# A four-bank rotation of the expert pre-activations in PSUM, sharing two banks with the mask broadcast

## The chip, the cores and the metric

The kernel runs on the 8 NeuronCores of one Trainium2 chip, as two dies of four cores each. Every core gets two of the sixteen sequences, that is 4096 rows of 1024 features, and all the weights; the cores exchange nothing. The metric is the device time in microseconds (us) of the slowest core, lower is better. TensorE is called PE below, its weight load PEld, VectorE DVE, ScalarE ACT, GpSimd POOL and SyncE, which issues most of the DMAs, SP.

## What is computed

The layer is a gated linear recurrence beside a mixture-of-experts feed-forward block with four experts and a hard choice of one for each token. Cut to what matters here:

```python
xn = layernorm(x)
s = xn + recurrence(rmsnorm(xn))              # forget / input / output projections, scan over time
logits = xn @ W_router
expert_idx = argmax(logits)                   # one of E = 4 experts for each token
h = einsum('th,ehi->tei', xn, W1) + b1        # H = 1024, I = 4096
h = gelu(h)
intermediate = einsum('te,tei->ti', onehot(expert_idx), h)
y = layer_norm(intermediate @ Wo + bo + xn)
out = x + s * silu(y)
```

## The kernel before

A core works in two blocks. Block A (the first 750 us or so) casts the weights to bf16 in DRAM, normalizes, projects, scans, and stores xn and s in bf16. Block B does the feed-forward part and is where the change is. It works through NT = 8 tiles of TT = 512 tokens, with features on partitions and tokens on the free axis.

The hard choice is turned into masking of the input: `maskedA` holds four copies of the tile's xn, copy e multiplied by the 0/1 mask of expert e, so that one accumulation over 4 experts x 8 slices of the features gives the pre-activation of the chosen expert. For each of IC = 32 slices of the 4096 intermediate features, called **groups** below (index `i_abs`), PE runs 32 matmuls of 128x128 by 128x512 (L621) and one matmul of 4 rows that adds the bias through the masks `mask4_bf` (L628), all into one PSUM bank, `pre[b]` with `b = i_abs % 2`. ACT reads that bank with one Gelu into `interA` (L784). The semaphore `pre_R<b>` counts finished groups of a bank (PE to ACT), `pre_F<b>` counts finished Gelus (ACT to PE): PE may start group i when the Gelu of group i-2 is done. The group's 1 MB of W1 comes through `w1sl`, two slots, loaded by SP.

After the 32 groups of tile t, PE runs `mask_prep(t + 1)`, which makes the masks of the next tile: four small transposes into `pmb2` (L588); DVE copies the result to `mask4_bf` (L717, in `mask_block`), after waiting for the last group of the tile; two matmuls (L594, L596) spread the masks of experts 0 and 1 over all partitions in `pmb` and `pmb2`; ACT copies both to `mb_bf` (L766, L767, in `mb_evacs`); then the same for experts 2 and 3 (L599, L601; L769, L770). Only then does PE start the second matrix product of tile t (L642, 8 output slices of 32 matmuls, accumulated in `y2a` and `y2b` in turn), which reads all of `interA`. DVE meanwhile builds `maskedA` of the next tile (L723) and then follows y2 with casts and squares (L740, L742). Sums for the layer norm go through `pmu` and `psq` (L655, L660), and in the middle of the next tile's groups PE transposes the finished product back (`emit_ptr`, L571, L578).

Each engine runs its own instruction list strictly in the order written. ACT's list for a tile is: the 32 Gelus, with a square root ahead of group 4 (`sqrtp`) and eight Silus ahead of group 12 (`silup`), both for the tile before; a drain; `mb_evacs(t + 1)`; eight reads of y2 (L794). A bank of PSUM holds 512 fp32 values in each partition, and block B allocates eight of them: `pre0`, `pre1`, `y2a`, `y2b`, `pmu`, `psq`, `pmb`, `pmb2`. All eight are used, `pmb` and `pmb2` only in `mask_prep`.

In SP's list of a tile the 32 loads of `w1sl` wait for `sl_F` (a group's weights used up), the 8 of `wosl` for `wo_F`; the load of the xn after the next and with it the first two `w1sl` loads of a tile wait for the last y2 of the tile before.

Of the kernel before, what the change touches and what calls it, by code (L numbers as in the profile page):

```python
# [28 lines left out]
def build_core(debug=False):  # L29
# [24 lines left out]
    with es:  # L54
# [20 lines left out]
            "pj_R0", "pj_F0", "pj_R1", "pj_F1",  # L75
            "ss_o", "vb_R0", "vb_F0", "vb_R1", "vb_F1",
            "sv_s", "bar",
            "s_xb0", "s_xb1", "s_sb", "sl_R0", "sl_R1", "sl_F", "wo_R0", "wo_R1", "wo_F",
            "s_lgR", "sv_lgF", "sv_mtm", "s_mtR", "sv_m4", "s_mbR", "ss_mb", "sv_msk",
            "pre_R0", "pre_F0", "pre_R1", "pre_F1", "s_predone", "ss_int",  # L80
            "y2_R0", "y2_F0", "y2_R1", "y2_F1", "s_wodone", "ss_y3",
            "sv_y3bf", "mu_R", "mu_F", "sq_R", "sq_F", "sv_var", "ss_sqrt",
            "sv_z", "ss_g", "sv_p", "s_pdone", "sv_out", "st_out",
# [3 lines left out]
        def ti(instr, name, k=1):  # L87
            instr.then_inc(SM[name], k)
            return instr

        def W(eng, name, val):
            if val > 0:
                eng.wait_ge(SM[name], val)
# [378 lines left out]
        with contextlib.ExitStack() as esB:  # L472
# [31 lines left out]
            pmb2_bf = pmb2.bitcast(BF16)  # L504
            pmu_bf = pmu.bitcast(BF16)
            psq_bf = psq.bitcast(BF16)

            y3bf = p_bf
            y3sq = g_bf
# [4 lines left out]
            with nc.Block() as blockB:  # L514
# [47 lines left out]
                def _(te):  # L562
# [20 lines left out]

                    def mask_prep(tau):
                        W(te, "ss_mb", 2 * tau)
                        ins = None
                        for sub in range(SUB):
                            ins = te.transpose(  # L588
                                pmb2_bf[0:4, sub * 128:(sub + 1) * 128],
                                mask_all[:, (tau * SUB + sub) * E:(tau * SUB + sub + 1) * E],  # L590
                                ident_bf[:, :])
                        ti(ins, "s_mtR", 1)
                        W(te, "sv_m4", tau + 1)
                        te.matmul(pmb[:, :], sel_bf[:, 0:128], mask4_bf[:, :],  # L594
                                  start=True, stop=True)
                        ti(te.matmul(pmb2[:, :], sel_bf[:, 128:256], mask4_bf[:, :],  # L596
                                     start=True, stop=True), "s_mbR", 1)
                        W(te, "ss_mb", 2 * tau + 1)
                        te.matmul(pmb[:, :], sel_bf[:, 256:384], mask4_bf[:, :],  # L599
                                  start=True, stop=True)  # L600
                        ti(te.matmul(pmb2[:, :], sel_bf[:, 384:512], mask4_bf[:, :],  # L601
                                     start=True, stop=True), "s_mbR", 1)

                    mask_prep(0)
                    for t in range(NT):
                        W(te, "sv_msk", t + 1)
                        for grp in range(NG):
                            if grp == NG // 2 and t > 0:
                                emit_ptr(t - 1)
                            gi = t * NG + grp  # L610
                            W(te, "sl_R%d" % (gi % 2), 16 * (gi // 2 + 1))
                            for il in range(G):
                                i_abs = grp * G + il
                                b = i_abs % 2
                                pr = t * IC + i_abs
                                W(te, "pre_F%d" % b, pr // 2)
                                first = True
                                for e in range(E):
                                    for k in range(KC):
                                        off = ((k * E + e) * G + il) * 128  # L620
                                        ins = te.matmul(  # L621
                                            pre[b][:, :], w1sl[gi % 2][:, off:off + 128],
                                            maskedA[:, (e * KC + k) * TT:(e * KC + k + 1) * TT],
                                            start=first, stop=False)
                                        first = False
                                        if il == G - 1 and e == E - 1 and k == KC - 1:
                                            ti(ins, "sl_F", 1)
                                ti(te.matmul(pre[b][:, :],  # L628
                                             b1t_bf[:, i_abs * 128:(i_abs + 1) * 128],
                                             mask4_bf[:, :], start=False, stop=True),  # L630
                                   "pre_R%d" % b, 1)
# [35 lines left out]
                def _(v):  # L667
# [45 lines left out]

                    def mask_block(tau):
                        W(v, "s_mtR", tau + 1)
                        W(v, "pre_R1", 16 * tau)
                        ti(v.tensor_copy(mask4_bf[:, :], pmb2_bf[0:4, 0:TT]), "sv_m4", 1)  # L717
                        W(v, "ss_mb", 2 * (tau + 1))
                        W(v, "s_xb%d" % (tau % 2), 16 * (tau // 2 + 1))
                        ins = None  # L720
                        for e in range(E):
                            for k in range(KC):
                                ins = v.tensor_tensor(  # L723
                                    maskedA[:, (e * KC + k) * TT:(e * KC + k + 1) * TT],
                                    xn_b[tau % 2][:, k * TT:(k + 1) * TT],
                                    mb_bf[:, e * TT:(e + 1) * TT], OP.mult)
                        DR(v, "sv_msk")
# [22 lines left out]
                def _(sc):  # L750
# [22 lines left out]
                    for t in range(NT):  # L773
                        sc.drain()
                        W(sc, "y2_R1", 4 * t)
                        for i_abs in range(IC):
                            if i_abs == 4 and t > 0:
                                sqrtp(t - 1)
                            if i_abs == 12 and t > 0:
                                silup(t - 1)  # L780
                            b = i_abs % 2
                            pr = t * IC + i_abs
                            W(sc, "pre_R%d" % b, pr // 2 + 1)
                            ti(sc.activation(interA[:, i_abs * TT:(i_abs + 1) * TT],  # L784
                                             pre[b][:, :], AF.Gelu), "pre_F%d" % b, 1)
                        DR(sc, "ss_int")
                        if t + 1 < NT:
                            mb_evacs(t + 1)
                        W(sc, "st_out", 16 * t)
                        for h in range(KC):  # L790
                            wi_ = t * KC + h
                            b = h % 2
                            W(sc, "y2_R%d" % b, wi_ // 2 + 1)
                            ti(sc.activation(y3[:, h * TT:(h + 1) * TT], y2[b][:, :],  # L794
                                             AF.Identity, bias=bo_cm[:, h:h + 1]),
                               "y2_F%d" % b, 1)
                        DR(sc, "ss_y3")
# [39 lines left out]
```

## Time and profile before

| what | value |
|---|---|
| time, median of 2 runs | 3296.91 us (3293.29 and 3300.54) |
| the profiled execution: time | 3300.92 us |
| its span on the slowest core (core 4) | 3299.0 us |
| spans of the eight cores | 3267.0 to 3299.0 us |
| mean granted TensorE clock, by core | 0.948 to 0.955 of full speed |
| PE busy, share of the span | 88% |
| DVE, ACT, POOL busy | 21%, 14%, 6% |
| mean busy share of the 16 DMA engines in block B | about 40% |

All rows are of one execution, on its slowest core. The span runs from the first to the last instruction of that core. PE's matmuls are pipelined, so the duration of a single one (about 380 ns) is longer than the distance from one to the next (about 219 ns); distances between starts are what counts. The granted clock is 1.00 at 2.4 GHz and 0.50 at 1.2 GHz. An idle time is put down to the instruction that ended it.

### The profile page before, as it was taken

The numbers are of one execution on the slowest core, as the hardware profiler recorded it, in microseconds if no ns is written. First come the engines' busy times: TensorE is split into PE (matmuls) and PEld (weight loads), VectorE is DVE, ScalarE is ACT, GpSimd is POOL, SyncE is SP. The second block draws the span as 40 slices with busy tenths as digits, with TensorE's granted clock in tenths as the row PEclk, the third lists the DMA queues.
The fourth block names the chain that finished last, engine by engine and source line by source line (L and its number), as shares of the span: only waits on it lengthen the run. The fifth ranks groups of instructions, "written<-read, shape, count | busy, mean of one in ns | idle before, by whom it ended". The sixth has DMA issues, their size and how long they took to land.

```text
span 3299.0 us, 32665 instructions; the slowest of 8 cores (3267.0 to 3299.0 us)
## 1 busy us (share of the span) xinstructions
PE 2891.8 (88%) x13376; PEld 1266.9 (38%) x13376; DVE 705.2 (21%) x1289; ACT 470.1 (14%) x733; POOL 211.7 (6%) x285
## 2 busy tenths in 40 slices
PE   0247778786999999999999999999999999999994
PEld 0113333332444444344444444444444444444442
DVE  0326666662002200310121012002200210021003
ACT  1122222210001110011102011101110111102001
POOL 1015252400000000000000000000000000000000
PEclk9878889898999999999999999999999999999997
DMA  9999999904444444444354434443444444344432
GB/s 133 105 131 124 128 123 148 142 29 164 143 141 166 153 159 161 153 142 164 128 190 141 154 139 179 151 156 139 180 155 147 180 137 161 141 166 141 161 145 76
DMA packets 262385, 476.14 MB, mean 144 GB/s; under 512 B 204700, under 2 KB 204700, under 8 KB 216988
## 3 DMA queue, kind: packets, MB, share of 16 engines
q1 hardware_dynamic: 88640, 408.99, 37.8%
q0 software_dynamic: 173600, 65.07, 18.4%
q8 instruction: 109, 1.79, 0.2%
q14 instruction: 36, 0.29, 0.0%
HBM read 482.44 MB, written 81.79 MB: 171 GB/s over the span
## 4 chain that ended last, share of the span: by engine, by line
PE 73%; DVE 1%; ACT 1%; DMA 1%; issue 1%; DVEq 0%; ACTq 0%; SPq 0%; POOL 0%; POOLq 0%
PE pre L621 55%; PE y2a L642 7%; PE y2b L642 7%; PE pre L628 2%; DMA w1sl<-w1s 1%; PE pmu L655 0%; DVE y L674 0%; DVEq L96 0%; DVE y L678 0%; PE psq L660 0%; PE pmu L571 0%; DVE maskedA L723 0%; PE y2b L647 0%; PE y2a L647 0%; ACT g_bf L760 0%
## 5 line engine op out<-in xcount | busy, mean ns | idle before, releaser
L621 PE MATMUL pre<-maskedA,w1sl 128*128 128x512 bf16 x8192 | 1823.3, 381 | 15.8 <-DVEq L96 12.4
L621 PEld LDWEIGHTS pre<-maskedA,w1sl 128*128 128x128 bf16 x8192 | 784.2, 98 | 988.7 <-issue 88.6
L784 ACT ACTIVATE interA<-pre 128x512 bf16<-128x512 f32 x256 | 152.8, 597 | 1721.0 <-PE pre L628 1720.9
L642 PE MATMUL y2a<-interA,wosl 128*128 128x512 bf16 x1024 | 238.7, 394 | 1.1 <-ACTq L96 1.1
L642 PE MATMUL y2b<-interA,wosl 128*128 128x512 bf16 x1024 | 226.2, 379 | 0.0
L717 DVE COPY mask_bf<-pmb 4x512 bf16<-4x512 bf16 x8 | 3.3, 412 | 951.7 <-PE pmb L588 951.7
L162 POOL DMA_DIRECT2D w1s<-w x256 | 188.0, 776 | 277.9 <-issue 277.9
L456 PE MATMUL pj<-xn_fm,wfT 128*128 128x512 bf16 x512 | 127.1, 410 | 83.8 <-ACT f_fm L243 58.5
L558 POOL DMA_DIRECT2D out<-y x8 | 6.0, 745 | 2631.9 <-DVEq L96 2631.9
L417 PE MATMUL trA<-ident_bf,xn_tm 128*128 128x128 bf16 x256 | 34.5, 278 | 141.9 <-DVEq L96 105.3
L642 PEld LDWEIGHTS y2a<-interA,wosl 128*128 128x128 bf16 x1024 | 102.5, 101 | 133.5 <-issue 21.9
L456 PE MATMUL pj<-xn_fm,wiT 128*128 128x512 bf16 x512 | 125.8, 409 | 28.8 <-DVE v_bf L325 16.4
L642 PEld LDWEIGHTS y2b<-interA,wosl 128*128 128x128 bf16 x1024 | 100.2, 98 | 120.9
L740 DVE CAST p_bf<-y 128x512 bf16<-128x512 f32 x64 | 27.3, 427 | 452.2 <-ACT y L794 450.1
L456 PE MATMUL pj<-xn_fm,woT 128*128 128x512 bf16 x512 | 121.8, 402 | 0.0
L456 PEld LDWEIGHTS pj<-xn_fm,wfT 128*128 128x128 bf16 x512 | 52.5, 104 | 157.4 <-issue 107.7
L711 DVE TENSOR_TENSOR p_bf<-s_b,g_bf 128x4096 bf16<-128x4096 bf16 x8 | 18.3, 2292 | 385.2 <-ACT g_bf L760 385.2
L628 PE MATMUL pre<-mask_bf,b1t_bf 4*128 4x512 bf16 x256 | 98.3, 384 | 0.0
L723 DVE TENSOR_TENSOR maskedA<-xn_b,mb_bf 128x512 bf16<-128x512 bf16 x256 | 86.6, 423 | 35.0 <-ACT mb_bf L770 35.0
L456 PEld LDWEIGHTS pj<-xn_fm,wiT 128*128 128x128 bf16 x512 | 52.2, 104 | 98.6 <-issue 49.1
L417 PEld LDWEIGHTS trA<-ident_bf,xn_tm 128*128 128x128 bf16 x256 | 23.7, 127 | 147.8 <-issue 146.5
L700 DVE TENSOR_TENSOR y<-y,mu_rep 128x512 f32<-128x512 f32 x64 | 39.2, 686 | 185.0 <-ACT rstd_rep L755 185.0
(114 smaller groups left out, 1240.0 us busy)
## 6 DMA issues: line engine op xcount, KB each, us to landing
w1sl<-w1s SPq DMA_DIRECT2D x256, 1024.0 KB, 4.8
wosl<-wos SPq DMA_DIRECT2D x64, 1024.0 KB, 5.0
w1s<-w POOLq DMA_DIRECT2D x256, 128.0 KB, 14.2
x_a<-x SPq DMA_DIRECT2D x8, 2048.0 KB, 14.7
x_b<-x SPq DMA_DIRECT2D x8, 2048.0 KB, 16.8
out<-y POOLq DMA_DIRECT2D x8, 2048.0 KB, 7.8
wos<-wo POOLq DMA_DIRECT2D x8, 1024.0 KB, 46.3
xnbf_s<-xn_fm SPq DMA_DIRECT2D x8, 1024.0 KB, 23.6
```

The lines of the kernel that those rows point to most:

```text
L162: ti(g.dma_start(out=dst, in_=src), "gp_cst", 16)
L417: ins = te.transpose(trA[p_][:, sub * 128:(sub + 1) * 128], xn_tm[:, sub * D + k * 128: sub * D + (k + 1) * 128], ident_bf[:, :])
L456: ins = te.matmul(pj[b][:, :], wT[:, k * D + c * 128: k * D + (c + 1) * 128], xn2_fm[:, k * TT:(k + 1) * TT], start=(k == 0), stop=(k == K ...
L558: ti(g.dma_start(out=dsto, in_=srco), "st_out", 16)
L621: ins = te.matmul(pre[b][:, :], w1sl[gi % 2][:, off:off + 128], maskedA[:, (e * KC + k) * TT:(e * KC + k + 1) * TT], start=first, stop=False)
L628: ti(te.matmul(pre[b][:, :], b1t_bf[:, i_abs * 128:(i_abs + 1) * 128], mask4_bf[:, :], start=False, stop=True), "pre_R%d" % b, 1)
L642: ins = te.matmul(y2[b][:, :], wosl[wi_ % 2][:, ic * 128:(ic + 1) * 128], interA[:, ic * TT:(ic + 1) * TT], start=(ic == 0), stop=False)
L700: v.tensor_tensor(y3[:, k * TT:(k + 1) * TT], y3[:, k * TT:(k + 1) * TT], mu_rep[:, :], OP.subtract)
L711: ti(v.tensor_tensor(p_bf[:, :], s_b[:, :], gsl(0, KC), OP.mult), "sv_p", 1)
L723: ins = v.tensor_tensor(maskedA[:, (e * KC + k) * TT:(e * KC + k + 1) * TT], xn_b[tau % 2][:, k * TT:(k + 1) * TT], mb_bf[:, e * TT:(e + 1 ...
L740: v.tensor_copy(y3bf[:, h * TT:(h + 1) * TT], y3[:, h * TT:(h + 1) * TT])
L784: ti(sc.activation(interA[:, i_abs * TT:(i_abs + 1) * TT], pre[b][:, :], AF.Gelu), "pre_F%d" % b, 1)
```

## The change

The pre-activations rotate through four banks in place of two. The two added ones are `pmb` and `pmb2`, which the mask broadcast also uses, so waits are added that keep the two uses apart:

- PE and ACT take `b = i_abs % 4` and `pre4[b]`, with `pre_R0..3` and `pre_F0..3`, each counting 8 groups a tile. PE may start group i when the Gelu of group i-4 is done.
- `mask_prep(tau)` for tau > 0 waits, ahead of its first transpose, until all Gelus on `pmb` and `pmb2` of the tile before are done (`pre_F2`, `pre_F3` at 8 * tau). The last of them are the Gelus of groups 30 and 31.
- Groups 2 and 3 of each tile wait in addition until ACT has read all four mask broadcasts of the tile (`ss_mb` at 2 * (t + 1)).
- DVE's wait ahead of the copy to `mask4_bf` names the last group by its new semaphore (`pre_R3` at 8 * tau).

No matmul, activation, copy or DMA is added or removed. The semaphore `sl_R2` is declared and not used.

```diff
+            pre4 = [pre[0], pre[1], pmb, pmb2]
@@ mask_prep
                         W(te, "ss_mb", 2 * tau)
+                        if tau > 0:
+                            W(te, "pre_F2", 8 * tau)
+                            W(te, "pre_F3", 8 * tau)
@@ tensor, groups
-                                b = i_abs % 2
-                                pr = t * IC + i_abs
-                                W(te, "pre_F%d" % b, pr // 2)
+                                b = i_abs % 4
+                                pr4 = t * (IC // 4) + i_abs // 4
+                                W(te, "pre_F%d" % b, pr4)
+                                if b >= 2 and i_abs < 4:
+                                    W(te, "ss_mb", 2 * (t + 1))
...
-                                            pre[b][:, :], w1sl[gi % 2][:, off:off + 128],
+                                            pre4[b][:, :], w1sl[gi % 2][:, off:off + 128],
...
-                                ti(te.matmul(pre[b][:, :],
+                                ti(te.matmul(pre4[b][:, :],
@@ vector, mask_block
-                        W(v, "pre_R1", 16 * tau)
+                        W(v, "pre_R3", 8 * tau)
@@ scalar
-                            b = i_abs % 2
-                            pr = t * IC + i_abs
-                            W(sc, "pre_R%d" % b, pr // 2 + 1)
+                            b = i_abs % 4
+                            pr4 = t * (IC // 4) + i_abs // 4
+                            W(sc, "pre_R%d" % b, pr4 + 1)
                             ti(sc.activation(interA[:, i_abs * TT:(i_abs + 1) * TT],
-                                             pre[b][:, :], AF.Gelu), "pre_F%d" % b, 1)
+                                             pre4[b][:, :], AF.Gelu), "pre_F%d" % b, 1)
```

## Rows read from the trace of the kernel before

**Rows 1.** The page, busy time (share of the span) and instructions.

```profile
PE 2891.8 (88%) x13376; PEld 1266.9 (38%) x13376; DVE 705.2 (21%) x1289; ACT 470.1 (14%) x733; POOL 211.7 (6%) x285
```

**Rows 2.** The page's groups: count, busy us, mean ns, idle before, its releaser.

```profile
L621 PE MATMUL pre<-maskedA,w1sl 128*128 128x512 bf16 x8192 | 1823.3, 381 | 15.8 <-DVEq L96 12.4
...
L784 ACT ACTIVATE interA<-pre 128x512 bf16<-128x512 f32 x256 | 152.8, 597 | 1721.0 <-PE pre L628 1720.9
...
L740 DVE CAST p_bf<-y 128x512 bf16<-128x512 f32 x64 | 27.3, 427 | 452.2 <-ACT y L794 450.1
```

**Rows 3.** Waits of PE, 1081 to 3299 us: total us, times, longest.

```profile
PE pmu L655 <- DVEq L96: 16.2, 7, 2.4
...
PE pmb L599 <- ACT mb_bf L767: 8.1, 6, 1.6
...
PE pre L621 <- DMA w1sl<-w1s: 3.2, 3, 2.4
```

**Rows 4.** Timeline, end of tile 2's groups: start, us, instruction, [idle before, releaser].

```profile
1636.26 0.39 PE L588 MATMUL pmb<-ident_bf,mask_all 128*4 128x128 bf16 x4
1636.43 0.60 ACT L784 ACTIVATE interA<-pre 128x512 bf16<-128x512 f32 x1 [6.73 <-PE pre L628]
1636.82 0.41 DVE L717 COPY mask_bf<-pmb 4x512 bf16<-4x512 bf16 x1 [118.32 <-PE pmb L588]
...
1637.38 0.37 PE L594 MATMUL pmb<-mask_bf,sel_bf 4*128 4x512 bf16 x1 [0.73 <-DVE mask_bf L717]
...
1638.06 0.58 ACT L766 CAST mb_bf<-pmb 128x512 bf16<-128x512 f32 x1 [1.03 <-PE pmb L596]
1638.54 0.59 ACT L767 CAST mb_bf<-pmb 128x512 bf16<-128x512 f32 x1
...
1639.28 0.37 PE L599 MATMUL pmb<-mask_bf,sel_bf 4*128 4x512 bf16 x1 [1.31 <-ACT mb_bf L767]
...
1639.80 1.74 PE L642 MATMUL y2a<-interA,wosl 128*128 128x512 bf16 x4
```

**Rows 5.** Timeline of PE, groups 0 to 2 of tile 0.

```profile
784.31 0.38 PE L628 MATMUL pre<-mask_bf,b1t_bf 4*128 4x512 bf16 x1
784.62 7.08 PE L621 MATMUL pre<-maskedA,w1sl 128*128 128x512 bf16 x32
791.64 0.38 PE L628 MATMUL pre<-mask_bf,b1t_bf 4*128 4x512 bf16 x1
791.95 7.08 PE L621 MATMUL pre<-maskedA,w1sl 128*128 128x512 bf16 x32
```

**Rows 6.** Timeline of ACT around the Silus ahead of group 12.

```profile
1170.66 1.28 ACT L760 ACT_TABLE_LOAD   x1
...
1179.01 0.60 ACT L784 ACTIVATE interA<-pre 128x512 bf16<-128x512 f32 x1
```

**Rows 7.** Windows around a mask_prep: PE, PEld, DVE, ACT, POOL busy, PEclk, DMA, GB/s.

```profile
1011.80:1015.30 3.50, 1.46 (x9) 0.44 (x8) 0.41 (x1) 1.67 (x3) 0.00 (x0) 1.00 0.00 0
1015.40:1018.70 3.30, 3.30 (x9) 1.17 (x9) 1.91 (x6) 1.07 (x2) 0.00 (x0) 0.50 0.00 0
1018.80:1030.00 11.20, 11.20 (x54) 5.05 (x53) 9.84 (x29) 0.69 (x1) 0.00 (x0) 1.00 0.27 94
```

**Rows 8.** The chain that ended last: start, us, 32 matmuls of one accumulation.

```profile
1015.45 8.66 PE y2a L642 x32
1031.45 6.91 PE y2a L642 x32
...
1204.37 8.01 PE pre L621 x32
...
1326.84 9.96 PE y2a L642 x32
...
2883.10 8.38 PE y2a L642 x32
```

**Rows 9.** Timeline, end of tile 1's groups: the first transposes of mask_prep.

```profile
1322.59 0.39 PE L588 MATMUL pmb<-ident_bf,mask_all 128*4 128x128 bf16 x4
```

## What the change will do to the time

> **What bounds the kernel now.** I read the page first. PE is busy for 88% of the span and no other engine for more than 21% [rows 1], and the matmul of the groups, L621, is by far the largest part [rows 2]. So a change helps if it takes away idle time or slow time of PE, and hurts if it adds some. The second look is at what PE waits for. The reader is to see in the groups of the page that all 8192 matmuls of L621 had 15.8 us of idle time before them, and 12.4 of that is the start of block B, where DVE builds the first masks [rows 2]. From 1081 us on, seven of the eight tiles, the waits of L621 are 3.2 us in three places, all for a weight DMA [rows 3]. None names ACT: PE never waits for a Gelu. ACT, on the other side, idles 1720.9 us before its 256 Gelus, waiting for PE, and a Gelu takes 597 ns [rows 2]. In the timeline a group starts 7.33 us after the one before (784.62 to 791.95) [rows 5]. A Gelu ends 0.77 us after the next work of PE has begun (1636.43 + 0.60 against 1636.26) [rows 4]; with two banks it could end some 6.4 us later than that before it held PE (7.33 - 0.77 - 0.15 for PE to wake, a figure worked out below).
>
> The third look is at the one place in the tile where PE, ACT and DVE hand work to each other in turn: the end of the groups [rows 4]. At 1636.26 PE is already in the transposes of `mask_prep`, and the last Gelu of the tile starts at 1636.43, beside them. Then DVE copies (1636.82), PE waits 0.73 us for it and runs the first broadcast, ACT reads twice, PE waits 1.31 us, runs the second broadcast, and y2 starts at 1639.80. From L588 to y2 it is 3.54 us, and every step hangs on the one before. This happens seven times, at the end of tiles 0 to 6. The fourth look is at the clock there: in the 3.5 us of handing over PE is busy for 1.46 us at a granted clock of 1.00; the 3.3 us behind it, y2 already running without a pause, show 0.50 (1.2 GHz), and then it is 1.00 (2.4 GHz) again [rows 7]. The chain shows the price: the first 32 matmuls of y2 take 8.66 us where 32 at full clock take 6.91, and once, at 1326.84, they take 9.96 [rows 8].
>
> **The change part by part.**
>
> *Four banks in place of two.* This lets ACT be up to three groups behind. The largest delay of a Gelu in a tile is behind the Silus: the table load starts at 1170.66 and Gelu 12 starts at 1179.01, 8.35 us of ACT's time [rows 6]. ACT has 6.73 us of idle time between two Gelus [rows 4], so Gelu 12 comes 8.35 - 6.73 = 1.6 us later than it otherwise would, and it may come 6.4 us later. So the trace has a deepest delay of ACT that two banks already swallow. The gain is 0 us: there is no wait of this kind to remove [rows 3].
>
> *More or other waits between groups.* Between a bias matmul and the next group there are 0.31 us (784.31 to 784.62) where the matmuls of a group are 0.22 us apart: 0.1 us for each of 256 boundaries. If that were the price of a bank's semaphore, it could move. But at 784.62 group 1 starts without any wait on `pre_F` (its value is 0, so none is issued), and at 791.95 group 2 starts with one, and both are 0.31 us behind their bias matmul [rows 5]. A wait that is already fulfilled costs nothing that can be seen, so I cost the sixteen added waits on `ss_mb` (groups 2 and 3 of 8 tiles) at 0. Their condition is met long before: ACT's four mask reads are over when y2 has barely begun, eight accumulations of 6.91 us [rows 8], so more than 50 us, earlier. If each did cost a whole such 0.1 us, it would be 1.6 us in all.
>
> *The wait at the head of `mask_prep`.* This one isn't fulfilled when PE comes to it. The Gelu of group 31 starts at 1636.43 and ends at 1637.03 [rows 4]. How long PE needs to wake after an ACT instruction is in the same rows: L767 ends at 1639.13, L599 starts at 1639.28, so 0.15 us. The transposes would then start at 1637.18 in place of 1636.26, **0.92 us later**. Queued behind the waiting transposes on PE are the two broadcasts and all of y2. DVE's copy waits for the transposes, ACT's reads wait for the broadcast (ACT idles 1.03 us before L766, so it isn't late itself), so the whole chain of 3.54 us shifts by 0.92 us and nothing in it is made shorter. Before, this Gelu lay beside the transposes and DVE's copy and cost nothing; now its cover is gone. Is there slack behind? The masks for the next tile come 0.92 us later, but DVE idles 450.1 us in total for results of y2 [rows 2], so its backlog is made good within y2. The wait of L655 at the end of y2 (up to 2.4 us) [rows 3] is for DVE's work on the last slice, so it hangs on y2's own end and shifts with it; the same holds for SP's loads of `xn_b` and the first `w1sl`, which wait for the last y2. No slack, so 7 x 0.92 = **6.4 us**.
>
> *The slow stretch behind it.* The pause grows from 3.54 to 4.46 us. What the clock then does is no row of before, so it is bounded. Seven first accumulations of y2 stand in the chain, 8.38 to 9.96 us, that is 1.5 to 3.05 us over 6.91; six are within 8.38 to 8.70, one is the 9.96 [rows 8]. The least I can find behind a pause is the one after `emit_ptr`'s short transposes: 8.01 us [rows 8] against the usual 7.02 (784.62 to 791.64) [rows 5], 1.0 us. I read it so that part of the slow time falls in the pause, where nothing runs that it could slow. If all boundaries went this way, six would get back 0.75: -4.5 us. If all went as at 1326.84, six would lose 9.96 - 8.66 = 1.3 each: +7.8 us. The one row of 9.96 has a longer pause ahead of it (1326.84 - 1322.59 = 4.25 us) [rows 8, 9], which makes the upper side the nearer one for a pause of 4.46. But a tile takes longer now, so the fall comes at another point of the pause in each tile, and both will be seen. I take one or two more of the long sort: **+2 us**.
>
> *Sum.* 6.4 + 2 = 8.4 us over the profiled execution's 3300.92 us: 3309.3. That execution lay 4.0 us above the median of the runs shown, 3296.91, so against the median it is 3305.3, rounded to **3305 us**, 0.25% slower. Nothing within 2% (66 us) can be told from no change in the measurement of this kernel, so this counts as no change.
>
> **The rivals.**
>
> 1. *It costs nothing on net.* The clock gives back what the pause takes: the extra pause is 6.4 us, the bound above for the give-back 4.5 us, and the two runs lie 7 us apart. The time would be 3297 to 3299 us. For it: the slow stretch costs less wherever it begins early in a pause. Against it: the row with the longest pause has the longest slow time. Chance 0.13.
>
> 2. *Faster: the boundary between groups shrinks.* If the 0.1 us beyond the usual distance came from the bank being too recently read, a rotation twice as long would take it away: 256 x 0.1 = 26 us less, less the 8 of above, gives 3279 us. Against it: groups 0 to 2 of tile 0 go to fresh banks and show the same 0.31 us [rows 5]. Even this is not 2%. Chance 0.03. For more than 2% there is no idle time on PE of that kind anywhere in the waits; 0.01.
>
> 3. *Slower by over 2%: the clock falls inside the groups.* The banks of the groups are now four, and PE goes to a new one every 7.33 us. Should this open pauses between groups that bring the clock to 0.50, each fall costs about 8.66 - 6.91 = 1.75 us. It takes 66 / 1.75 = 38 falls in 256 groups to decide; one in each turn of the rotation, 64, would give 112 us, and 3296.9 + 8 + 112 = 3417 us. Against it: the two-bank rotation changes banks just as often, and its clock is 1.00 outside the pauses [rows 7]. Four banks change neither the count of the changes nor the fulfilled waits. Chance 0.03. The Trainium skill ("TensorE: Matmul & The Clock Gate", section "A second HAM failure mode: psum-queue depth-cycling") describes a kernel with 512 columns that goes through the PSUM banks in turn, whose TensorE idles briefly between groups so often that its clock goes up and down; by that rule this rival would be likely. The rows of this case don't bear it out for two banks, and none shows four.
>
> **How the numbers follow.** Forecast (slower by 3 to 20 us) 0.80, rival 1 0.13, rival 2 0.04 with its remote end, rival 3 0.03. The bounds: the low end is the median plus 6.4, less 4.5 for the clock and less 3.6 for half the distance of the runs, 3295; rival 1 lies inside, and I go to 3294. The high end is the median plus 6.4 plus 7.8 plus 3.6, 3315, and 3 us for the stretch behind `emit_ptr`, whose slow time can move too: 3318. Rivals 2 and 3 are left out, 0.07, and the rest is for tails. Faster by over 2%: 0.01. Within: 0.96. Slower: 0.03.
>
> **What would show it.** Right: a new wait of PE in `mask_prep`'s transposes for the Gelu, seven times, some 0.8 to 0.9 us each, and those transposes starting about 1.2 us behind the last bias matmul in place of 0.3; from there to y2 3.5 us as before; 7.33 us from group to group; no wait of L621 for ACT, as before; a Gelu of 597 ns; first accumulations of y2 between 8.0 and 10 us, with perhaps two or three near 10. Wrong: L621 at a distance other than 7.33 us, a granted clock below 1.00 inside the groups, waits of groups 2 or 3 for `ss_mb`, or a start of the transposes that isn't later. If the pauses grow by 0.9 us and the time still doesn't, the clock's part was mis-sized.

## The result

| | before | changed |
|---|---|---|
| median of the undisturbed runs | 3299.5 us (11 runs, 3293.3 to 3308.4) | 3315.7 us (8 runs, 3312.0 to 3320.1) |
| ratio, 95% interval | | 1.0049 (1.0037 to 1.0061): 12 to 20 us slower |
| profiled execution, span of the slowest core | 3299.0 us (core 4) | 3321.9 us (core 7) |
| block B, median of the eight cores | 2543.2 us | 2559.2 us |

One die of the chip is disturbed in some executions of either kernel (here 3511 us and more); those are left out. The ratios below are each taken against runs of the kernel before on the same chip; the medians of the kernel before on the three chips used lie between 3299 and 3301 us. Block B and everything cut out of it come from one profiled execution of each kernel, eight cores each, partly on different chips. How far such figures scatter shows in experiment 1: a difference of 2 us in block B or in one stage of it can be chance.

The last line needs a word, since it carries much of what follows. Block A ends at a different time on every core and in every execution (between 698 and 770 us over all the profiles of this study), and this has nothing to do with the change. Block B is counted from the first transposes of `mask_prep` to the end of the core's span, and there the cores agree to a few us. It can be read off the view of that line, here of the changed kernel's slowest core (duration ns min/median/max, first and last start):

```profile
L592 PE MATMUL pmb<-ident_bf,mask_all x32: 216/217/314, 749.3 to 2888.5; 128*4 128x128 bf16 x32
```

3321.9 - 749.3 = 2572.6 us for this core; the eight lie between 2554.3 and 2584.9, those of before between 2542.5 and 2553.6. The two longest of the changed kernel are cores 6 and 7, which the last section is about; the medians hardly feel them.

### The profile page after: what moved, and what is told of

Read it like the earlier page. It is cut to its first block, busy times and chain, and to the rows that moved or that the text cites. A ratio compares the mean times of both kernels' runs of the same rounds, so it can differ in the third digit from the quotient of the medians.

```text
span 3321.9 us, 32693 instructions; the slowest of 8 cores (3285.2 to 3321.9 us)
## 1 busy us (share of the span) xinstructions
PE 2908.1 (88%) x13376; PEld 1267.5 (38%) x13376; DVE 706.2 (21%) x1289; ACT 470.9 (14%) x733; POOL 211.4 (6%) x285
## 3 DMA queue, kind: packets, MB, share of 16 engines
q0 software_dynamic: 173600, 65.07, 18.5%
## 4 chain that ended last, share of the span: by engine, by line
PE 72%; DMA 2%; DVE 2%; ACT 1%; issue 1%; DVEq 0%; SPq 0%; ACTq 0%; POOL 0%; POOLq 0%
PE pre L627 27%; PE pmb L627 27%; PE y2a L648 7%; PE y2b L648 7%; DMA w1sl<-w1s 1%; PE pmb L634 1%; PE pre L634 1%; DVE y L684 0%; DVE y L680 0%; DVEq L96 0%; DMA wosl<-wos 0%; DVE maskedA L729 0%; PE y2b L653 0%; PE y2a L653 0%; PE pmu L572 0%
## 5 line engine op out<-in xcount | busy, mean ns | idle before, releaser
L627 PE MATMUL pre<-maskedA,w1sl 128*128 128x512 bf16 x4096 | 916.7, 382 | 19.3 <-DVEq L96 12.4
L627 PE MATMUL pmb<-maskedA,w1sl 128*128 128x512 bf16 x4096 | 909.0, 380 | 0.0
L627 PEld LDWEIGHTS pre<-maskedA,w1sl 128*128 128x128 bf16 x4096 | 393.4, 98 | 509.9 <-issue 62.9
L627 PEld LDWEIGHTS pmb<-maskedA,w1sl 128*128 128x128 bf16 x4096 | 390.9, 98 | 484.2 <-issue 37.4
L648 PE MATMUL y2a<-interA,wosl 128*128 128x512 bf16 x1024 | 248.4, 405 | 1.1 <-ACTq L96 1.1
L790 ACT ACTIVATE interA<-pmb 128x512 bf16<-128x512 f32 x128 | 76.6, 598 | 864.5 <-PE pmb L634 864.5
L790 ACT ACTIVATE interA<-pre 128x512 bf16<-128x512 f32 x128 | 76.6, 598 | 861.8 <-PE pre L634 861.7
L717 DVE TENSOR_TENSOR p_bf<-s_b,g_bf 128x4096 bf16<-128x4096 bf16 x8 | 18.3, 2292 | 385.4 <-ACT g_bf L766 385.4
## 6 DMA issues: line engine op xcount, KB each, us to landing
w1s<-w POOLq DMA_DIRECT2D x256, 128.0 KB, 18.5
```

Of the source, the lines that this page charges most:

```text
L627: ins = te.matmul(pre4[b][:, :], w1sl[gi % 2][:, off:off + 128], maskedA[:, (e * KC + k) * TT:(e * KC + k + 1) * TT], start=first, stop=False)
L648: ins = te.matmul(y2[b][:, :], wosl[wi_ % 2][:, ic * 128:(ic + 1) * 128], interA[:, ic * TT:(ic + 1) * TT], start=(ic == 0), stop=False)
L717: ti(v.tensor_tensor(p_bf[:, :], s_b[:, :], gsl(0, KC), OP.mult), "sv_p", 1)
L790: ti(sc.activation(interA[:, i_abs * TT:(i_abs + 1) * TT], pre4[b][:, :], AF.Gelu), "pre_F%d" % b, 1)
```

## The profile after

The waits of PE from 1060 us on (total us, times, longest), slowest core, changed kernel:

```profile
PE pmb L603 <- ACT mb_bf L773: 8.2, 6, 1.6
PE pre L627 <- DMA w1sl<-w1s: 6.8, 6, 2.0
PE pmb L592 <- ACT interA L790: 5.0, 6, 0.8
...
PE y2b L648 <- DMA wosl<-wos: 0.8, 2, 0.6
```

Against [rows 3] there is one new row, `pmb L592 <- ACT interA L790`: the transposes of `mask_prep` wait for the Gelu, here six times, and with the hand-over before 1060 us seven times for 5.9 us in all. No row names a Gelu as what L627, the matmul of the groups, waits for, as before. The wait for ACT's mask reads (L603) is what it was. The waits for weights are larger.

The end of tile 2's groups in the timeline, which answers to [rows 4]:

```profile
1631.16 0.38 PE L634 MATMUL pmb<-mask_bf,b1t_bf 4*128 4x512 bf16 x1
1631.64 0.60 ACT L790 ACTIVATE interA<-pmb 128x512 bf16<-128x512 f32 x1 [6.73 <-PE pmb L634]
...
1632.38 0.38 PE L592 MATMUL pmb<-ident_bf,mask_all 128*4 128x128 bf16 x4 [0.84 <-ACT interA L790]
1632.94 0.41 DVE L723 COPY mask_bf<-pmb 4x512 bf16<-4x512 bf16 x1 [118.69 <-PE pmb L592]
...
1633.50 0.37 PE L598 MATMUL pmb<-mask_bf,sel_bf 4*128 4x512 bf16 x1 [0.73 <-DVE mask_bf L723]
...
1635.40 0.58 PE L603 MATMUL pmb<-mask_bf,sel_bf 4*128 4x512 bf16 x1 [1.31 <-ACT mb_bf L773]
...
1635.78 0.63 PE L605 MATMUL pmb<-mask_bf,sel_bf 4*128 4x512 bf16 x1
...
1636.34 1.46 PE L648 MATMUL y2a<-interA,wosl 128*128 128x512 bf16 x3
```

The transposes start 1.22 us behind the last bias matmul (1631.16 to 1632.38); before it was 0.31. From there DVE's wait (0.73) and ACT's (1.31) are the same to the hundredth. New behind them: L603 and L605 take 0.58 and 0.63 us where the matmul of [rows 4] takes 0.37, and y2 starts 3.96 us behind the transposes and not 3.54. The clock has fallen before the hand-over is over. The windows of the same place (columns as in [rows 7]):

```profile
1632.40:1634.60 2.20, 0.95 (x6) 0.30 (x6) 0.41 (x1) 0.42 (x1) 0.00 (x0) 1.00 0.00 0
1634.70:1641.40 6.70, 6.00 (x14) 1.94 (x15) 3.66 (x11) 1.63 (x4) 0.00 (x0) 0.50 0.00 0
1641.60:1660.00 18.40, 18.40 (x87) 8.32 (x85) 9.02 (x25) 1.38 (x2) 0.00 (x0) 1.00 0.34 115
```

The granted clock is 0.50 (1.2 GHz) for at least 6.7 us, twice as long as in [rows 7], and then 1.00 again. In the chain that ended last the first accumulation of y2 now takes

```profile
1636.40 9.54 PE y2a L648 x32
```

and the seven of them are 9.33, 9.66, 9.54, 9.71, 9.78, 8.43 and 9.61 us, one short and six long, where before one was long [rows 8].

**Where the 16 us are.** I cut each core's block B into the same five stages for the seven cycles from one hand-over to the end of the next tile's groups, by the starts of PE's matmuls in the timeline, and took the mean over the eight cores (us, sum of seven):

| stage | before | changed | difference |
|---|---|---|---|
| last bias matmul to the transposes | 2.2 | 8.6 | +6.4 |
| transposes to the end of y2's first 32 matmuls | 86.7 | 92.4 | +5.7 |
| the rest of y2 | 349.0 | 349.5 | +0.5 |
| end of y2 to the next tile's first group (the sums) | 58.9 | 60.9 | +2.0 |
| 32 groups, with `emit_ptr` | 1683.7 | 1685.1 | +1.4 |
| sum | 2180.5 | 2196.5 | +16.0 |

The second line is the slow clock. Over 8 cores there are 56 hand-overs; y2's first 32 matmuls end 12.1 us (12.4 in three cases) behind the transposes where the slow stretch is short and 13.2 to 14.1 us where it is long. Long ones are 8 of 56 before and 43 of 56 in the changed kernel. The fourth line holds a wait that I had not counted, for the first weights of a tile: PE's waits for `w1sl` and `wosl` add up to a median of 3.6 us a core before and 7.6 us after. The first two lines are far outside the scatter. The last three aren't: `banks_only` of experiment 1, whose hand-over is that of before, has 60.9 us in the fourth line too.

## The experiments

**1. The wait alone, and the banks alone.** Two kernels split the change. The first keeps two banks and adds only the wait:

```diff
                     def mask_prep(tau):
                         W(te, "ss_mb", 2 * tau)
+                        if tau > 0:
+                            W(te, "pre_F0", 16 * tau)
+                            W(te, "pre_F1", 16 * tau)
```

> Two banks as before; only the wait is added: mask_prep's transposes wait for all Gelus of the tile (pre_F0, pre_F1). My theory (the whole loss is the wait and what the clock does behind it): as the changed kernel, 1.0049 times before, +13 to +19 us; transposes 1.22 us behind the last bias matmul, five to seven of the seven hand-overs followed by a long slow stretch (first accumulation of y2 ends 13.2 us or more behind the transposes in place of 12.1). Rival R1 (rotating through four banks costs by itself, about half of the 16 us): at most +8 us. Rival R2 (the wait is hidden, noise): +0 us.

Measured: 1.0040 (1.0027 to 1.0053) times before, block B 2561.7 us (+18.5). Long slow stretches in 49 of 56 hand-overs. Its five stages are 8.6, 93.5, 349.5, 60.9 and 1683.7 us, 2196.1 in all, where the changed kernel has 2196.5. The second takes the changed kernel's rotation through four banks, but over banks that no one needs at the hand-over, so the wait falls away:

```diff
-            pre4 = [pre[0], pre[1], pmb, pmb2]
+            pre4 = [pre[0], pre[1], y2[0], y2[1]]
...
-                        if tau > 0:
-                            W(te, "pre_F2", 8 * tau)
-                            W(te, "pre_F3", 8 * tau)
...
-                                    W(te, "ss_mb", 2 * (t + 1))
+                                    W(te, "y2_F%d" % (b - 2), 4 * t)
```

> Four banks, the two added ones are y2a and y2b in place of pmb and pmb2, so mask_prep needs no new wait; groups 2 and 3 wait for ACT's last reads of y2, long fulfilled. My theory: the same as before within 0.1% (3 us), at most one or two long slow stretches in the seven hand-overs, as before. R1: about +8 us or more. If a deeper rotation helped at all (a gain hidden in the changed kernel by the wait): below before, by 3 us or more.

Measured: 1.0013 (0.9992 to 1.0033), block B 2545.2 us (+2.0), 13 long stretches of 56. The wait by itself does all that the change does, and four banks by themselves do nothing that can be told from zero, in either direction. The total of this kernel alone would still allow the +8 us of R1 (its interval ends at +11 us); block B, the full loss in `wait_only` and the next experiment, whose interval ends at +5 us, rule it out. A hidden gain of 3 us or more lies just outside the interval.

**2. The order of the four banks.** The changed kernel with its list turned round:

```diff
-            pre4 = [pre[0], pre[1], pmb, pmb2]
+            pre4 = [pmb, pmb2, pre[0], pre[1]]
```

with the waits renamed accordingly (`pre_F0`, `pre_F1` ahead of `mask_prep`, `ss_mb` ahead of groups 0 and 1).

> The changed kernel with the order of its four banks turned round: pmb and pmb2 take groups 0, 1, 4, 5, ..., 28, 29; pre0 and pre1 take groups 30 and 31. mask_prep now waits for the Gelus of groups 28 and 29, done some 6.5 us before PE comes there. My theory: all of the 16 us come back, the time is that of before within 3 us, transposes 0.31 us behind the last bias matmul. R1 (rotation): +8 us stays. A third theory, sharing banks with the mask broadcast costs through something else than this wait: +16 us stays.

Measured: 1.0002 (0.9990 to 1.0014), block B 2544.4 us (+1.2), 14 long stretches. The same place in PE's timeline (slowest core):

```profile
1634.53 0.38 PE L634 MATMUL pre<-mask_bf,b1t_bf 4*128 4x512 bf16 x1
1634.85 0.38 PE L592 MATMUL pmb<-ident_bf,mask_all 128*4 128x128 bf16 x4
...
1638.38 2.24 PE L648 MATMUL y2a<-interA,wosl 128*128 128x512 bf16 x5
```

The transposes are 0.32 us behind the bias matmul again and y2 3.53 us behind them. All waits are still in the program, but the last Gelu that they ask for, of group 29, ended at 1620.96, 13.9 us before PE comes to the transposes:

```profile
1620.36 0.60 ACT L790 ACTIVATE interA<-pmb 128x512 bf16<-128x512 f32 x1 [6.73 <-PE pmb L634]
```

(The 6.5 us of the expectation are those of group 30's Gelu, which isn't waited for.) So it isn't the sharing of `pmb` that costs but which groups are the last to use it.

**3. The clock by itself.** Filler matmuls, whose results nobody reads, give PE something to do in the pauses. They write `y2a`, and a wait on `y2_F0` makes sure that ACT has read it. The edit of the changed kernel:

```diff
+                    def fill(tau, n):
+                        for _ in range(n if tau > 0 else 0):
+                            te.matmul(y2[0][:, :], ident_bf[:, :],
+                                      xn_b[(tau - 1) % 2][:, 0:TT],
+                                      start=True, stop=True)
...
                         if tau > 0:
+                            W(te, "y2_F0", 4 * (tau - 1))
+                        fill(tau, 4)
+                        if tau > 0:
                             W(te, "pre_F2", 8 * tau)
...
+                        fill(tau, 3)
                         W(te, "sv_m4", tau + 1)
...
+                        fill(tau, 6)
                         W(te, "ss_mb", 2 * tau + 1)
```

In the kernel before the four ahead of the transposes are left out.

> The changed kernel with filler matmuls in PE's three pauses of mask_prep (4 ahead of the transposes, 3 ahead of the first broadcast, 6 ahead of the second; each 128x512, about 0.22 us, into y2a, whose content is overwritten later). They are meant to be no longer than the pauses. My theory (the clock's part is about 9 to 10 of the 16 us, the pause's 6.4): granted clock 1.00 through the hand-over and behind it, the first accumulation of y2 in 6.9 us, so 7 x 1.7 to 3.1 us = 12 to 20 us less than the changed kernel: 3 us below before to 5 us above it, -3 to +5. Rival (the slow stretch has another cause than PE's idleness): no gain, still about +16 us.

> The kernel before with the same filler matmuls in the two pauses it has in mask_prep (3 ahead of the first broadcast, 6 ahead of the second; none ahead of the transposes, where it does not wait). It measures the two terms apart: against after_filled only the wait itself differs, so after_filled minus before_filled is 7 x 0.9 = 6.3 us (0.2%); against before only the slow stretch behind the hand-over differs, 7 x 1.7 and one or two long ones, so 0.9955 to 0.9970 times before, -10 to -15 us, and granted clock 1.00 behind the hand-over. Rival: if the wait and not the clock carried the whole loss, before_filled would be the same as before and after_filled 16 us above it.

Measured: `after_filled` 1.0000 (0.9981 to 1.0018), block B 2540.9 us; `before_filled` 0.9986 (0.9963 to 1.0008), block B 2532.3 us. In both, all 56 hand-overs are alike: y2's first 32 matmuls end 10.5 to 10.7 us behind the transposes, and the clock does not fall. The windows of `before_filled` around its first hand-over:

```profile
1005.00:1012.00 7.00, 7.00 (x34) 2.51 (x33) 0.41 (x1) 2.22 (x5) 0.00 (x0) 1.00 0.00 0
1012.00:1015.50 3.50, 3.50 (x18) 1.61 (x17) 2.80 (x9) 0.53 (x2) 0.00 (x0) 1.00 0.00 0
1015.50:1030.00 14.50, 14.50 (x69) 6.53 (x68) 10.07 (x28) 1.37 (x2) 0.00 (x0) 1.00 0.43 146
```

Three things follow. The fall is caused by PE's idleness: no real work was moved, and it is gone. With the clock held up, the two kernels differ by 2540.9 - 2532.3 = 8.6 us in block B (6.6 in the sum of the stages), near the 7 x 0.97 = 6.8 us by which their pauses differ (the transposes are 1.28 us behind the bias matmul with the filler there, 0.31 without). And the changed kernel wins 18.3 us by the filler, about what its 56 hand-overs say (13.20 - 10.52 = 2.7 us each, 7 x 2.7 = 18.8). For the kernel before it didn't come out as expected. The hand-overs give 7 x (12.38 - 10.52) = 13 us, but block B gets only 10.9, and the total isn't clear of zero. PE's waits for weights are a median of 13.3 us a core there, against 3.6, and the clock falls in the sums in 11 of 56 cases, against 49. So the sums themselves became shorter too, and all of that and a little more went into waiting for a DMA: the stage is 60.2 us, against 58.9.

**4. The wait for weights.** How that comes about stands in PE's timeline of the kernel before, at the end of tile 0 and at the end of tile 1, slowest core:

```profile
1076.27 3.11 PE L655 MATMUL pmu<-p_bf,ones_bf 128*128 128x512 bf16 x8 [2.09 <-DVEq L96]
1079.18 2.40 PE L660 MATMUL psq<-g_bf,ones_bf 128*128 128x512 bf16 x8
1081.93 2.32 PE L621 MATMUL pre<-maskedA,w1sl 128*128 128x512 bf16 x10 [0.36 <-DMA w1sl<-w1s]
...
1389.23 1.89 PE L655 MATMUL pmu<-p_bf,ones_bf 128*128 128x512 bf16 x8 [2.35 <-DVEq L96]
1390.96 1.89 PE L660 MATMUL psq<-g_bf,ones_bf 128*128 128x512 bf16 x8
1395.27 7.07 PE L621 MATMUL pre<-maskedA,w1sl 128*128 128x512 bf16 x32 [2.42 <-DMA w1sl<-w1s]
```

Where the clock falls at the sums, L655 and L660 take 5.3 us and the weights are nearly there; where it doesn't, they take 3.6 us and PE waits 2.42 us. The first weights of a tile are asked for only after the last y2, because on SP the load of `xn_b`, which has to wait for it, stands ahead of them. Moved behind the second weight load:

```diff
-                        if t + 1 < NT:
-                            W(sy, "y2_R1", 4 * t)
-                            W(sy, "sv_msk", t)
-                            ti(sy.dma_start(out=xn_b[(t + 1) % 2][:, :], ...
                         for grp in range(NG):
+                            if grp == 2 and t + 1 < NT:
+                                W(sy, "y2_R1", 4 * t)
+                                W(sy, "sv_msk", t)
+                                ti(sy.dma_start(out=xn_b[(t + 1) % 2][:, :], ...
```

> The kernel before with one change on SP: the load of xn_b moves from ahead of a tile's first weight load to behind the second, so w1sl's first two loads no longer wait for the last y2. It prices the weight waits of the kernel before: PE waits for w1sl and wosl a median of 3.6 us a core from 1060 us on. Theory: those go, and nothing else does, 3 to 4 us less (0.999 times before), also within the hand-over nothing changes. Rival: the xn_b load, now later, holds DVE up, or the clock at the sums takes it back: +-0 or slower.

> The changed kernel with the same move of the xn_b load. My three-term account of the +16 us in block B is 6.3 (the wait) + 5.7 (longer slow stretches behind the hand-over) + 4.0 (more waiting for weights: median 7.6 us a core against 3.6). If the third term is real, the changed kernel loses its 7.6 us here, and against before_loads_first it is 6.3 + 5.7 = 12 us slower, not 16: about 1.0025 times before. Rival: the weight waits are only another face of the clock (where they go, the clock falls instead) and after_loads_first stays 16 us above before_loads_first.

Measured: `before_loads_first` 0.9979 (0.9962 to 0.9997), block B 2539.5 us, 3.7 less, waits for weights 0.1 us. That is the expected size, but not only by the waits: against the table of before the stages are 6.1 us shorter in the mean of the cores, 4.3 in the sums and 1.7 at the hand-over, where no stretch is long any more. `after_loads_first` 1.0012 (0.9997 to 1.0027), block B 2548.6 us, 10.6 less, waits 0.3. Between the two it is 9.1 us, less than the 12 I expected. The five stages place it:

| stage, sum of seven, us | before_loads_first | after_loads_first | difference |
|---|---|---|---|
| last bias matmul to the transposes | 2.2 | 8.6 | +6.4 |
| transposes to the end of y2's first 32 | 85.0 | 92.7 | +7.7 |
| the rest of y2 | 349.2 | 349.3 | +0.1 |
| the sums | 54.6 | 51.6 | -3.0 |
| the groups, with `emit_ptr` | 1683.4 | 1682.1 | -1.3 |
| sum | 2174.4 | 2184.2 | +9.8 |

(In `after_loads_first` 46 hand-overs of 56 are long, in `before_loads_first` none.) The wait and the hand-over's slow clock are fully there, 14 us. With the weights no longer in the way, the sums and the groups give back 4.3 us of it. In the changed kernel itself this gift could not be had: the time that the sums saved went into waiting for weights. So the 4 us of waiting for weights were not a third cost standing beside the other two, as I had put it; it is what kept the changed kernel from the give-back. The traces also show what the give-back in the sums is: in `before_loads_first` the clock falls at the sums in all 56 cases, and the stage takes 7.8 us; in `after_loads_first` it doesn't in 15 of 56, and there it takes 6.2 us. 15 x 1.6 / 8 = 3 us a core, the whole of the line. Why the clock is spared more often there when the hand-over gets longer was not tested.

**5. A version without the hand-over.** The next tile's masks need not wait for the end of the groups. With two buffers for `mask4` the transposes go ahead of group 20, the broadcasts ahead of groups 23 and 26, and ACT's reads ahead of Gelus 25 and 28. PE then goes from the groups into y2 at once, waiting for the last two Gelus only at the matmuls that read them:

```diff
+                            if t + 1 < NT:
+                                if grp == 20:
+                                    mask_tr(t + 1)
+                                if grp == 23:
+                                    mask_bc(t + 1, 0)
+                                if grp == 26:
+                                    mask_bc(t + 1, 1)
...
-                        if t + 1 < NT:
-                            mask_prep(t + 1)
-                        W(te, "ss_int", t + 1)
...
+                                if h == 0 and ic == 0:
+                                    W(te, "pre_F1", 16 * t + 15)
+                                if h == 0 and ic == IC - 2:
+                                    W(te, "pre_F0", 16 * (t + 1))
+                                if h == 0 and ic == IC - 1:
+                                    W(te, "ss_int", t + 1)
```

> Two banks as before, but the next tile's masks are made inside the groups: transposes ahead of group 20, broadcasts ahead of groups 23 and 26, ACT's reads ahead of Gelus 25 and 28, two mask4 buffers; the second product waits for the last two Gelus only at its matmuls 30 and 31. The hand-over disappears from the end of the groups. My theory: per tile the two pauses (0.73 + 1.31) and the slow stretch (1.7 and a bit) go, 3.8 us x 7 = 27 us, so 0.9915 to 0.993 times before, -23 to -28 us; no fall of the clock at the start of y2. Rival: the work inside the groups opens pauses or another wait there (the mask reads hold up Gelus, DVE is late) and half or more of it is given back: -13 us or less.

Measured: 0.9891 (0.9864 to 0.9917), that is 27 to 45 us less; block B 2515.5 us, 27.7 less. The account had 27, but it is a balance: from the last bias matmul to the end of y2's first 32 it is 38.3 us less, as neither a pause nor a fall of the clock is left there; the groups, which now hold the mask matmuls, are 6.6 longer and the sums 3.1. Then fillers in the other two places where PE idles, 10 into `pmu` ahead of the sums, 1 to 3 into `y2a` in `emit_ptr`:

> masks_early, with filler matmuls in the other two places of a tile where PE idles and the clock falls: 10 ahead of the layer norm's sums (pause 2.1 to 2.4 us) and 1 to 3 in each of emit_ptr's pauses (0.72, 0.21, 0.34 us). My theory (the clock falls because PE idles, everywhere): the clock stays at 1.00 from the first group to the last tile; 8 x (1.6 to 1.8) us at the sums and 7 x 1.0 to 1.3 behind emit_ptr come on top of masks_early, 18 to 22 us more, so 0.985 to 0.988 times before. Rival: the clock falls there for another reason, or fillers push the real work back: no better than masks_early.

Measured: 0.9893 (0.9864 to 0.9923), no better in total, a miss. Block B is 2505.9 us, 9.6 less and not 18 to 22, and the waits for weights are 13.3 us a core where `masks_early` has 4.8. Nor is the clock at 1.00 throughout, as expected: one to four falls a core are left, 24 in all. Each begins within 1.3 us of the start of a tile's first group, and each of these groups has waited 2.0 to 3.3 us for its weights, as here on core 1:

```profile
1656.16 8.73 PE L643 MATMUL pre<-maskedA,w1sl 128*128 128x512 bf16 x32 [2.93 <-DMA w1sl<-w1s]
```

The group takes 8.73 us and not 7.07 or so. It is the same hand-on as in experiment 3, so experiment 4's move was added:

> masks_early_filled with the same move of the xn_b load. There the median wait for weights is 13.4 us a core, against 4.8 in masks_early: the fillers keep the clock up at the sums, and PE then reaches the first group of a tile before its weights. Theory: the 13 us go, so 0.985 times before (masks_early_filled had 0.9893), and block B is about 2493 us a core against 2505.9. Rival: the loads collide with other loads when issued early (wosl's last, x), and PE waits elsewhere: 0.989.

Measured: 0.9829 (0.9802 to 0.9855), block B 2485.2 us, 58 less than before and 20.7 less than without the move, where 13 were expected. No core shows a fall of the clock between the first group and the last tile; that the falls behind the waits are gone as well fits the 7 us on top. What is left of PE's waits from 1060 us on, slowest core:

```profile
PE pmu L578 <- DVE p_bf L737: 28.4, 1, 28.4
PE pmu L578 <- DVE y L700: 1.2, 3, 0.5
PE pre L643 <- DMA w1sl<-w1s: 0.7, 1, 0.7
PE y2a L667 <- DMA wosl<-wos: 0.3, 1, 0.3
PE pmu L681 <- DVEq L96: 0.3, 1, 0.3
```

The 28.4 us are the end of the program. This version is 1.7% (1.4 to 2.0) faster than the kernel before, and more than that against the changed one.

## Why the prediction was right, and where it was off

**That it would be a little slower, by the wait at the head of `mask_prep`: right.** The term was 7 x 0.92 = 6.4 us; the stage table has +6.4. The row that was named in advance is there, seven times at about 0.84 us. `wait_only` shows that this wait alone brings the whole loss, `swap_order` that the loss goes with it. The measured 3315.7 us lie inside the range, near its upper end; of the 10.7 us over the 3305 forecast 2.6 are the median of before, 3299.5 and not 3296.9 us. And a loss of half a percent can be told from no change here, against what was said of 2%: the interval starts at 1.0037.

**That four banks bring nothing: right.** ACT's lateness never reached PE, and `banks_only` is at 1.0013, its interval around 1. The groups are 7.33 us apart as before, so rival 2 is out (group 2 of tile 0, counted among those on fresh banks, is in fact the second use of `pre0`; its distance of 0.31 us spoke against the rival all the more), and the added waits on `ss_mb`, which `banks_only` replaces by others, cost nothing that shows.

**The clock behind the hand-over: right mechanism, mis-sized term.** I took one or two more long stretches of seven, +2 us, between bounds of -4.5 and +7.8. It was 43 of 56 in place of 8, +5.7 us. The step that failed is the count drawn from the sentence that the fall would come "at another point of the pause in each tile, and both will be seen". Both are seen, but the long sort is the rule. The one row of a long pause [rows 8, 9] was the nearest to the changed kernel's, and I gave it less weight than six rows with a shorter pause. I had also read its 4.25 us as if they were all pause. The timeline of the kernel before has them apart:

```profile
1324.66 0.58 ACT L766 CAST mb_bf<-pmb 128x512 bf16<-128x512 f32 x1 [1.31 <-PE pmb L596]
...
1325.88 0.54 PE L599 MATMUL pmb<-mask_bf,sel_bf 4*128 4x512 bf16 x1 [1.59 <-ACT mb_bf L767]
...
1326.22 0.63 PE L601 MATMUL pmb<-mask_bf,sel_bf 4*128 4x512 bf16 x1
...
1326.77 1.46 PE L642 MATMUL y2a<-interA,wosl 128*128 128x512 bf16 x3
```

ACT's read comes 0.28 us later than at the other tiles (1.31 for 1.03 us of idle time), which is real pause. The rest, some 0.4 us, is L599 and L601 running at the slow clock, as L603 and L605 do in the changed kernel: an effect of the fall and not its cause. The 0.28 us are there at tile 1 on all eight cores, and five of the 8 long stretches of before are at tile 1. That suggests that a little more pause already makes the long sort frequent. In the changed kernel the clock falls 1.9 to 3.1 us behind the transposes where the stretch is long, that is before y2 starts, and 3.1 to 3.7 us behind them where it is short. What else decides it is open: with an unchanged hand-over the long ones were 8 (before), 13 (`banks_only`), 14 (`swap_order`) and 0 (`before_loads_first`) of 56.

**"No slack, so 7 x 0.92": incomplete.** I had seen that SP's loads of a tile's first weights hang on the last y2, and concluded that they only shift along. They do, but whether PE waits for them depends on how long the sums take. The stage of the sums came out at +2.0 us, for which the forecast had no term; that these 2 us come from the change isn't shown, as `banks_only` has them too. `after_loads_first` against `before_loads_first` shows that without the waits the same stage would have given 3 us back.

So 8.4 us were forecast, and 16 us were measured. Of the 7.6 missing, 3.7 are the clock's term and 3.9 the three other stages, where scatter may have a part.

**Rival 3 (the clock falls inside the groups) did not happen**, apart from the 14 us on two cores in the last section, at another level. The Trainium skill ("TensorE: Matmul & The Clock Gate", section "A second HAM failure mode: psum-queue depth-cycling") describes a kernel with 512 columns that goes through the PSUM banks in turn and whose TensorE idles briefly between groups so often that its clock goes up and down. No run here shows it: `banks_only` has the groups at the same distance of 7.33 us, and its clock falls inside them only behind `emit_ptr`, as before. What the Trainium skill says on the same page in the section "HAM oscillation — how this bites in real kernels", that the work behind a wait of TensorE starts at the slow clock, the hand-over bears out, and the fillers show it; the waits there are for a DMA and 3 to 5 us long, here they are three, of 0.7 to 1.3 us each.

## What to carry to other kernels

Before two uses share a PSUM bank, ask which instruction uses the bank last ahead of the hand-over: giving the last turns of the rotation to other banks made a 16 us loss vanish with every wait still in place. A hand-over of 3.5 us that grew by 0.9 us cost nearly as much again behind it, in slow clock (6.4 and 5.7 us over seven), so pauses at a serial hand-over are best taken apart (early masks) or filled. And price a gain by what comes next: twice here much of what a faster clock gave was lost again in waiting for a weight load, and once the load was moved too, it was kept.

## What had not been expected of the hardware

In the changed kernel's profiled execution the last tile's y2 ran slow on cores 6 and 7, in a third way. Two windows of core 7 there:

```profile
3200.00:3260.00 60.00, 58.91 (x228) 24.36 (x227) 6.17 (x12) 4.73 (x7) 0.00 (x0) 0.83 0.33 118
...
3208.00:3279.00 71.00, 68.11 (x259) 27.87 (x257) 8.70 (x17) 5.51 (x8) 0.00 (x0) 0.81 0.29 104
```

PE is busy for 68.1 of 71 us, and the granted clock is 0.81, neither 0.50 nor 1.00 (the first window holds some time at 1.00); the chain has 8.40 us for 32 matmuls there, where 6.91 are usual. It costs these two cores 11 to 13 us of span, and they are the slowest of that execution. For 14 us the level is there in the last tile's groups too (0.81 from 3124 to 3138 us on core 7). The same level stands in two other places of the profiles, both in block A: on cores 4 and 5 of this execution (0.81 from 240 to 286 us on core 5) and on cores 6 and 7 of `masks_early_filled`. The stage table ends ahead of the last tile's y2, so it isn't part of the 16 us. No experiment was made on it.
